# Attention and a mixture of experts on one core: products with V two units at a time, and one PSUM bank moved from maxima to probability scores

## The reference, cut to what matters

```
c_kv = x @ W_DKV                      # 64 latent columns
k, v = c_kv @ W_UK, c_kv @ W_UV       # 16 heads of 16
q = x @ W_UQ
scores = where(causal, q k^T / sqrt(16), -inf)
ctx = softmax(scores) @ v
```

## Time and profile before

| | us |
|---|---|
| median of 3 runs (lowest, highest) | 1200.76 (1198.31, 1200.98) |
| profiled execution, its own time | 1197.37 |
| its span, first to last instruction | 1195.6 |
| busy: PE, DVE, ACT, POOL | 1048.3, 782.2, 494.0, 386.1 |
| mean granted TensorE clock | 0.921 |

### The profile page before, as it was taken

How to read it: one execution, slowest core, us unless ns; L and a number is a source line. 1 busy time by engine, 2 the same in 40 slices (tenths; PEclk the granted TensorE clock), 3 DMA queues, 4 the chain that set the end, 5 groups by cost and what they waited for, 6 DMA issues and landing times. The chain is left out here.

```text
span 1195.6 us, 19608 instructions
## 1 busy us (share of the span) xinstructions
PE 1048.3 (88%) x5364; PEld 538.1 (45%) x5365; DVE 782.2 (65%) x2352; ACT 494.0 (41%) x1043; POOL 386.1 (32%) x721
## 2 busy tenths in 40 slices
PE   6898399999999999999865762499999999999995
PEld 2344023333333333333245652266666666666663
DVE  5665399989989998999126874155555555555552
ACT  2334037777777777777821231122222222222221
POOL 2223613333333333333230567122222222222222
PEclk9888569999999999999988875699999999999998
DMA  2664983665555534530038773122232222222222
GB/s 84 206 199 162 207 169 98 131 140 140 119 117 117 117 82 97 97 69 20 21 102 279 243 245 133 49 36 47 48 48 45 44 44 44 45 48 46 44 46 26
DMA packets 102396, 121.22 MB, mean 101 GB/s; under 512 B 26352, under 2 KB 81776, under 8 KB 102320
## 3 DMA queue, kind: packets, MB, share of 16 engines
q1 hardware_dynamic: 89024, 102.55, 33.7%
q0 software_dynamic: 13296, 17.77, 8.9%
HBM read 70.27 MB, written 49.63 MB: 100 GB/s over the span
## 5 line engine op out<-in xcount | busy, mean ns | idle before, releaser
L640 ACT ACTIVATE b_prob<-b_prob_ps 128x512 f32<-128x512 f32 (+3 forms) x768 | 319.7, 503 | 100.0 <-PE b_prob_ps L684 96.5
L596 DVE CUSTOM_DVE_ANT_0 b_max_ps<-b_max_ps,b_mask_max 128x256 f32<-128x256 f32 (+3 forms) x512 | 245.7, 500 | 49.1 <-PE b_max_ps L666 49.0
L666 PE MATMUL b_max_ps<-b_k_st,b_q_st 96*128 96x512 bf16 (+3 forms) x768 | 248.9, 345 | 25.0 <-DMA b_k_st<-k_parts 22.0
L684 PE MATMUL b_prob_ps<-b_q_st,b_k_st 99*128 99x512 bf16 (+3 forms) x768 | 241.2, 330 | 10.2 <-ACT b_prob L640 8.9
L554 POOL TENSOR_SCALAR_AFFINE_SELECT b_prob<-b_prob 128x128 f32<-128x128 f32 x512 | 141.8, 292 | 310.4 <-ACT b_prob L640 297.3
L1354 POOL DMA_INDIRECT out_dram<-e_y,e_token x71 | 110.1, 1551 | 326.2 <-DVE e_y L1408 310.4
L599 DVE TENSOR_REDUCE b_neg_max<-b_max_ps 128x1 f32<-128x512 f32 x256 | 176.0, 687 | 9.4 <-PE b_max_ps L666 8.0
L705 PE MATMUL b_acc_ps<-b_prob,b_v_aug 128*32 128x512 f32 (+3 forms) x1536 | 163.3, 498 | 0.0
L666 PEld LDWEIGHTS b_max_ps<-b_k_st,b_q_st 96*128 96x128 bf16 x768 | 74.8, 99 | 179.7 <-DVE b_neg_max L596 68.7
L1461 PE MATMUL e_g_ps<-w_sb,e_rowsT 128*128 x284 | 135.5, 600 | 0.4 <-issue 0.4
L1461 PE MATMUL e_a_ps<-w_sb,e_rowsT 128*128 x284 | 134.1, 595 | 0.0
(11 more groups left out here) (164 smaller groups left out, 1062.0 us busy)
## 6 DMA issues: line engine op xcount, KB each, us to landing
w_sb<-in_L_ffn_W SPq DMA_DIRECT2D x11, 1024.0 KB, 11.8
e_rows<-slot_rows SPq DMA_DIRECT2D x72, 129.0 KB, 2.1
ctx_cols<-b_ctx_out SPq DMA_DIRECT2D x16, 512.0 KB
q_parts<-a_part_q SPq DMA_DIRECT2D x8, 768.0 KB, 3.8
k_parts<-a_part_k SPq DMA_DIRECT2D x8, 768.0 KB, 4.2
b_q_st<-q_parts SPq DMA_DIRECT2D x16, 384.0 KB, 5.0
b_k_st<-k_parts SPq DMA_DIRECT2D x16, 384.0 KB, 7.7
a_x<-in_L_attn_x SPq DMA_DIRECT2D x8, 512.0 KB, 6.3
```

What stands on the lines that cost most here:

```text
L596: nc.vector.tensor_tensor_reduce(scores, scores, mask_max[:, HALF - width:HALF], -1.0, -MASKED, ALU.add, ALU.min, to).then_inc(max_done, 1)
L640: nc.scalar.activation(prob[n % NP][:, 0:width], prob_ps[n % NS][:, 0:width], ACT.Exp, scale=SCALE).then_inc(prob_ok, 1)
L666: nc.tensor.matmul(out[:, 0:width], q_st[g % RING][0:STACK, h, i * P:(i + 1) * P], k_st[g % RING][0:STACK, h, half * HALF:half * HALF + wi ...
L684: nc.tensor.matmul(prob_ps[n % NS][:, 0:width], k_st[g % RING][0:MAXROWS, h, j * P:(j + 1) * P], q_st[g % RING][0:MAXROWS, h, q0:q0 + widt ...
```

## The change

TensorE issues the products of two units one behind the other, at the end of each odd unit's step, not those of one unit at the end of each step; the even unit's products so come one step later. Of the seven banks for scores the maxima have three instead of four and the probability scores four instead of three. Everything else follows from these numbers: the waits of `bank_free` and of `prob_scores`, and the bank into which the maxima are turned.

```
-    NM, NS = 4, 3
+    NM, NS = 3, 4
...
-                if unit - LEAD - LAG >= 0:
-                    products(unit - LEAD - LAG)
+                if unit - LEAD - LAG >= 0 and unit % 2:
+
+                    for back in (1, 0):
+                        products(unit - LEAD - LAG - back)
```

## The result

The changed kernel takes 1229.29 us in the median (1228.91 to 1232.57), the kernel before 1200.87: 2.2% slower, ratio 1.0224 with a 95% interval of 1.0185 to 1.0262. The forecast was 1223, slower, in a range of 1207 to 1231.

A forecast was written before the change was run, and what follows sets the result against it. TensorE was taken to bound the kernel before; after the change, VectorE's chain would set pairs. 23.8 (quads) + 1.8 (joints) - 3.1 (tail) = +22.5 us on 1197.4 gives 1220, with 3.4 for the median 1223; range 1207 to 1231.

The forecast's parts named there:

- one sum: Attention, each pair of units: latencies, five VectorE reductions and two products in a chain; 29.15 us a quad against 27.45.
- the draw: Rival for attention: first starts and releases overlap better than read, +0.2 us a quad, 1201 us; chance 0.09.
- Pairing saves TensorE's gaps: Attention's product calls: a pair pays one 0.24 us gap instead of two, gaining 0.22 a pair, 21 us at most.
- a joint: Border between two product calls run back to back: about 0.02 us each, 1.8 us for 88 of them.
- B: First of a quad's six pairs of units, eight maxima scores of 512 columns: 5.77 us, against 4.50 before.
- The dense rival: Rival for attention: VectorE never holds TensorE, so quads save 18 us and the tail 3, 1180 us; chance 0.09.
- The tail: End of attention, without maxima: four banks for probability scores shorten eight pairs by 3.1 us, bounds 1 to 4.
- The lead: Start of attention, sixteen units of maxima alone at VectorE's pace: 0 us change, at most +2.
- D, E, F and A: Third to sixth pairs of units in a quad: forecast 4.41, 3.82, 6.05 and 5.32 us.
- The phase after attention: Stretch between attention and the experts: the prediction's sum had no term for it.
- The sum for attention: Whole attention phase: 23.8 for quads, 1.8 for joints, 3.1 off in the tail, together +22.5 us.
- The clock rival: Rival for attention: TensorE's pauses lower its clock; a tenth of the phase falling adds 30 us, 1250; chance 0.04.

The follow-up runs named there:

- e3: Changed kernel with VectorE taking each maximum over only half of the block's columns: 1173.99 us, ratio 0.9751 to the kernel before.
- e4: Kernel before with VectorE taking each maximum over only half of the block's columns: 1201.79 us against 1203.86.
- e1: Kernel before with only the banks moved, three for maxima and four for probability scores, products single: 1200.22 us against 1203.86, ratio 0.9979.
- e2: Kernel before with only the products paired, four banks for maxima and three for probability scores: 1212.3 us, ratio 1.0071.
- e10: Kernel before with all seven banks as one ring in TensorE's order and products paired: 1212.92 us, ratio 1.0101.

## Why the prediction was right

**The bound of a pair.** The forecast rested on one sum: first score to VectorE, five reductions, release, last score pair, two products. It held in each of six pairs within 0.12 us, and e3 against e4 shows that VectorE's chain is its cause. VectorE is idle at the start of all six, so no backlog of it crosses their borders, and the draw's +0.2 a quad was +1.7. e1 and e2 show that it takes both edits for the full loss: 27.46 with neither, 27.31 and 28.02 with one, 29.16 with both.

**Pairing saves TensorE's gaps.** This part was right and even a little better than put: a joint costs nothing that can be seen, not 0.02. In B 896 columns and the way out take 1.64 us from 403.20 to 404.84, and 1.493 + 0.147 is 1.64. The 1.8 us that the sum had for joints do not exist; so it had 25.6 for the quads, where 23.8 were measured. The Trainium skill (TensorEngine Tiling, Key Properties) has it that a change of tiling mode drains TensorE. The trace fits that, with a gap of some 0.10 us ahead of the 16 records, 0.15 behind them and none between the two calls; but the products differ from the scores in type as well (float32 and bf16), so it does not show that the tiling is the reason. The gain comes out where VectorE is relieved: the quad of e3, with both edits, is 25.79, and that of e4, with neither, 27.44. In the changed kernel VectorE's chain is longer by more.

**The dense rival** (1180) fell by the result, and e2 and e10 show that more banks don't save it: with four, or seven shared, the burst still waits, for ScalarE or for VectorE.

**The tail was mis-sized:** -1.6, not -3.1. I took 0.41 us as the pitch of an exponential at 512 columns from four that took 1.85. That unit mixes 512 and 384. In the changed kernel's tail eight exponentials of a pair of 512 take 4.03:

```profile
614.12 4.03 ACT L640 ACTIVATE b_prob<-b_prob_ps 128x512 f32<-128x512 f32 x8 [1.39 <-PE b_prob_ps L684]
617.95 0.69 ACT L614 ACTIVATE b_ctx_out<-b_acc_ps 128x512 f32<-128x512 f32 x1
618.43 4.13 ACT L640 ACTIVATE b_prob<-b_prob_ps 128x512 f32<-128x512 f32 x8
```

(4.03 - 0.61) / 7 is 0.49; the 0.61 is the duration of one of them. With 0.49 the eighth score of two units of 512 comes at 2.55 and the pair at 4.71 instead of 4.48. The sum also left out the copy of the accumulator (L614), which stands between the two groups of eight and takes 0.48 us of ScalarE's time there. Here is the start of the pair with eight scores of 512 and two products of 512, and that of the pair after it, in the changed kernel, and then its start in the kernel before (it ends at 597.66):

```profile
617.35 1.24 PE L684 MATMUL b_prob_ps<-b_q_st,b_k_st 99*128 99x512 bf16 x4
...
622.83 1.80 PE L684 MATMUL b_prob_ps<-b_q_st,b_k_st 99*128 99x512 bf16 x6
```

```profile
592.17 1.18 PE L684 MATMUL b_prob_ps<-b_q_st,b_k_st 99*128 99x512 bf16 x3
```

This pair, for which the sum had 4.48 in place of 4.8, takes 5.48 us where it took 5.49. ScalarE now runs without a gap from 614.12 to 622.56, the end of the pair's exponentials, so that what TensorE saves doesn't show. The tail's gain comes from the other pairs.

**The lead** stood at zero, with +2 at most, and was +2.2. Of these 0.7 come before the first transpose (164.9 against 164.2) and 1.5 between it and the second. In that stretch maxima and products run together in four pairs already, D, E, F and A, which the count of 14 full quads leaves out. By the forecast's own sums E, F and A add 0.4, and they did (15.22 us against 14.85). The other 1.1 come ahead of them, and no run shows why.

**The phase after attention** stood at zero in the sum and was +7.3 between the two traces. With it the terms are 23.8 + 2.2 - 1.6 + 7.3 = 31.7, the difference of the spans. The medians are 28.4 apart, of which attention explains 24.4; the other 4.0 are open.

**What was luck.** The sum for attention, +22.5, lies near the 24.4 measured partly because two errors cancel: 1.8 too much for joints and 1.5 too much gained in the tail.

**The clock rival:** attention kept its 1.00 in every stretch shown after its lead. The clock did move, in a phase that the change doesn't touch.

## What to carry to other kernels

Before one engine's work is put together to spare it gaps, count how long it then stays away from its consumers. In pair B the eighth score starts at 402.82 and the next pair's first at 404.84, 2.0 us later, and VectorE starts on that another 0.27 us later. Three reductions at 0.61 last 1.8 us, so VectorE runs out of work. Each such burst then costs the way from TensorE to VectorE, the reductions that the ring makes TensorE wait for (five of eight, with three banks), and the way back. Sum that chain from rows for each width, since the dense engine's busy share doesn't show it.

With single products one ring over all seven banks, in the producer's order, was worth more than the two splits that were measured: a quad of 26.92 us against 27.46 (4 and 3) and 27.31 (3 and 4). With paired products it was not: 28.28 against 28.02 (4 and 3).

## What the runs showed of the hardware that was not expected

Between attention and the experts TensorE's mean granted clock was 0.66 to 0.72, between its two levels, and some 457 matmuls that the change doesn't touch stretched over 156.0 to 163.9 us, the longer the lower the clock was, but for 158.0 at 0.70 and 157.7, twice, at 0.69. One profiled execution of this kernel against another can therefore be off by 0.6%. The stretch that a change touches, and medians over several runs, are the safer comparisons. And two calls of products in column groups follow each other without any gap: 896 columns and the way out took 1.64 us.
